# A two-layer decoder kernel: the first layer's expert weights loaded once each, and copied into one working block for every tile of tokens

## What is computed

```python
# E = 8 experts, TOP_K = 2, D = 256, H = 512, x: 2048 tokens of 256
logits = x @ Wg                       # [tokens, 8]
w, pick = softmax over the two largest logits of each token
y = sum over the two picks k:  w[k] * ( (silu(x @ W1[e]) * (x @ W2[e])) @ W3[e] ),  e = pick[k]
out = layernorm(x + y)
```

## Time and profile before

| what | value |
|---|---|
| median of 3 runs | 1277.59 us (1275.09 to 1281.85) |
| the profiled execution, its own time | 1270.34 us |
| its span, first to last instruction | 1268.3 us |
| TensorE busy | 1009.9 us (80%) |
| VectorE, ScalarE, GpSimd busy | 578.7 us, 356.5 us, 228.8 us |
| bytes moved by DMA | 129.22 MB |
| granted TensorE clock, mean | 0.892 of full speed |

### The profile page before, as it was taken

The page is one execution under the profiler, slowest core; times in us unless marked ns, Lnnn a source line. Parts: engine busy times, 40 slices in busy tenths (PEclk is TensorE's granted clock), DMA queues, the critical chain, the costliest instruction groups (busy, mean ns, idle before and its releaser), DMA issues.

```text
span 1268.3 us, 19930 instructions
## 1 busy us (share of the span) xinstructions
PE 1009.9 (80%) x8500; PEld 761.2 (60%) x8500; DVE 578.7 (46%) x1328; ACT 356.5 (28%) x491; POOL 228.8 (18%) x234
## 2 busy tenths in 40 slices
PE   6889689889888888887875797988879797974860
PEld 3656566656657777776874564756556474643540
DVE  3544343545683411111113825565473649445227
ACT  2344324433442121111110153242315322430112
POOL 0310210210302222323221010101010110102642
PEclk9899789988988999999997897999699789966995
DMA  5012912012005778767662000200020010004426
GB/s 168 2 38 97 347 42 67 1 38 67 1 1 215 282 282 303 269 249 258 253 254 83 1 6 2 67 2 5 1 67 2 5 34 1 2 1 128 148 90 198
DMA packets 68216, 129.22 MB, mean 102 GB/s; under 512 B 12752, under 2 KB 57696, under 8 KB 63136
## 3 DMA queue, kind: packets, MB, share of 16 engines
q1 hardware_dynamic: 45984, 97.85, 22.5%
q10 hardware_dynamic: 16480, 14.62, 3.6%
q0 software_dynamic: 5664, 15.47, 3.4%
HBM read 94.50 MB, written 33.42 MB: 101 GB/s over the span
## 4 chain that ended last, share of the span: by engine, by line
PE 52%; DVE 22%; DMA 13%; ACT 6%; POOL 2%; issue 2%; SPq 1%; ACTq 1%; DVEq 0%; POOLq 0%
DMA sb_arena<-in_m_w 11%; PE ps L1627 7%; PE ps L1324 6%; PE ps L1443 6%; DVE sb_arena L793 6%; PE ps L1509 4%; PE ps L1419 4%; ACT sb_arena L587 4%; DVE sb_arena L797 3%; PE ps L1637 3%; DVE ps L816 3%; PE ps L1562 3%; PE ps L1465 2%; PE ps L1701 2%; PE ps L1451 2%
## 5 line engine op out<-in xcount | busy, mean ns | idle before, releaser
L1627 PE MATMUL ps<-sb_arena 128*128 128x128 f32 x1248 | 161.1, 284 | 44.0 <-DMA sb_arena<-in_m_w 43.3
L1627 PEld LDWEIGHTS ps<-sb_arena 128*128 128x128 f32 x1248 | 151.4, 198 | 56.9 <-DMA sb_arena<-in_m_w 55.6
L1214 POOL TENSOR_TENSOR sb_arena<-sb_arena,sb_neghalf 128x2 f32<-128x2 f32 x40 | 30.5, 762 | 602.4 <-DVE sb_arena L759 602.4
L587 ACT ACTIVATE sb_arena<-ps 77x2048 f32<-77x2048 f32 (+1 forms) x64 | 118.4, 1875 | 54.6 <-PE ps L1401 42.0
L1324 PE MATMUL ps<-sb_arena,sb_wreg 128*128 128x256 f32 (+1 forms) x512 | 107.9, 363 | 4.6 <-issue 3.8
L1324 PEld LDWEIGHTS ps<-sb_arena,sb_wreg 128*128 128x128 f32 (+1 forms) x512 | 89.2, 195 | 19.7 <-issue 8.3
L1419 PE MATMUL ps<-sb_arena 32*77 32x256 f32 (+1 forms) x1024 | 92.5, 491 | 7.7 <-ACT sb_arena L587 4.9
L1112 DVE COPY sb_arena<-ps 128x256 f32<-128x256 f32 x39 | 16.6, 424 | 161.2 <-PE ps L1621 161.2
L822 DVE RECIPROCAL sb_arena<-ps 128x32 f32<-128x32 f32 x24 | 8.6, 357 | 147.0 <-PE ps L1451 146.0
L1637 PE MATMUL ps<-sb_arena 128*128 128x256 f32 x312 | 73.9, 380 | 0.6 <-ACT sb_arena L688 0.6
L1273 POOL DMA_INDIRECT outs<-sb_arena,sb_idx x39 | 38.3, 983 | 196.4 <-ACT sb_arena L688 196.4
(11 more groups left out here) (228 smaller groups left out, 1710.1 us busy)
## 6 DMA issues: line engine op xcount, KB each, us to landing
sb_arena<-in_m_w SPq DMA_DIRECT2D x39, 1536.0 KB, 7.1
sent<-sb_xres SPq DMA_DIRECT2D x32, 256.0 KB, 2.9
sb_arena<-outs SPq DMA_DIRECT2D x16, 512.0 KB, 5.8
outs<-sb_zeros ACTq DMA_DIRECT2D x1, 6656.0 KB, 32.7
sent<-sb_zeros ACTq DMA_DIRECT2D x2, 2560.0 KB, 12.7
sb_arena<-in_m_w SPq DMA_DIRECT2D x16, 256.0 KB, 3.7
early<-sb_xres SPq DMA_DIRECT2D x12, 256.0 KB, 2.9
sb_arena<-in_xT SPq DMA_DIRECT2D x8, 256.0 KB, 3.3
```

The lines of the kernel that those rows point to most:

```text
L587: nc.scalar.activation(dst, src, ACT.Exp).then_inc(S(f"h_PT{p}"), 1)
L1627: ins = mm(to[:, m * P:(m + 1) * P], w[:, k, m * P:(m + 1) * P], slots0[j % 2].xT[:, k, :], start=(k == 0), stop=(k == KC - 1))
```

## The change

All eight experts' blocks stay in SBUF. `arena` is cut into blocks of 3072 words: eight of them hold the experts (`BLOCKS`, in the order of first use), one (number 6) is the working block from which PE reads every tile's weights, one (number 1) holds the two sets of `xT`, `sil` and `hT`.

- SyncE issues eight loads in a row, each with a register load of the expert's number from `first_i`; the last four wait also for `h_res1`. The second layer's weights follow in one piece after the first tile's W3.
- The table is now made in two parts: `uses()` in `table_early()` ranks the experts by first use (and then come those without a tile), and `blocks_early()`, a new step of the list behind `index`, makes the table of block numbers, `block_i`.
- For every tile ScalarE copies W1 and W3 and VectorE copies W2 from the expert's block into the working block, 1024 words a row each, with a register load of the block's number ahead of each copy. The copy of W1 for tile j+1 waits until PE has done W1(j), that of W2 until W2(j) is done, that of W3 for tile j until W3(j-1) is done. PE waits for `t_c1`, `t_c2` and `t_c3` in place of the DMA.
- The first copies wait until the last pair's result has been copied away (`store` at 8), as do VectorE's first steps of the mixture.
- Two small constants (`expert_no`, `blocks`) are loaded at the start, on ScalarE's queue.

```diff
-WBUFS = 3
+WORDS = 3072
+BLOCKS = (2, 3, 4, 0, 7, 8, 9, 5)
+EARLY_BLOCKS = 4
+WORK, ROWS = 6, 1
...
-                           "res": [("index",)], "rstd": [("gather",)]} if last else {})
+                           "res": [("index",), ("blocks",)], "rstd": [("gather",)]} if last else {})
...
             sp.wait_ge(S("h_res0"), X0.at(PAIRS))
             sp.wait_ge(S("placed"), 1)
-            for j in range(WBUFS):
-                load_weights(j)
+            sp.wait_ge(S("table"), 1)
+            for k, blk in enumerate(BLOCKS):
+                if k == EARLY_BLOCKS:
+                    sp.wait_ge(S("h_res1"), X0.at(PAIRS))
+                e = sp.value_load(first_i[0:1, k:k + 1], min_val=0, max_val=E - 1)
+                sp.dma_start(arena[:, WORDS * blk:WORDS * (blk + 1)], dram["m0_w"][bass.ds(e, 1), :, :].rearrange("e p a -> (e p) a")
+                             ).then_inc(S(f"landed{k}"), 16)
             for p in range(2):
                 send(p, PAIRS - 1, 0)
-            later = [n for n, _ in attn_items("s1") + attn_items("x1")]
-            for j in range(TILES0 - 2):
-                if j + WBUFS < TILES0:
-                    sp.wait_ge(S("t_y"), j + 1)
-                    load_weights(j + WBUFS)
-                if later:
-                    load_weight(sp, later.pop(0), "c_weights")
+            sp.wait_ge(S("t_y"), 1)
+            for n, _ in attn_items("s1") + attn_items("x1"):
+                load_weight(sp, n, "c_weights")
...
+            def weights0(j, part, used, signal):
+
+                if j < E:
+                    act.wait_ge(S(f"landed{j}"), 16)
+                if j:
+                    act.wait_ge(S(used), j)
+                act.wait_ge(S("table"), 3 if j >= SURE else 2)
+                blk = act.value_load(block_i[0:1, j:j + 1], min_val=0, max_val=max(BLOCKS))
+                nc.scalar.activation(arena[:, WORDS * WORK + 1024 * part:WORDS * WORK + 1024 * (part + 1)],
+                                     arena[:, bass.ds(blk * WORDS + 1024 * part, 1024)], ACT.Copy).then_inc(S(signal), 1)
+
+            act.wait_ge(S("store"), B)
+            weights0(0, 0, "t_u", "t_c1")
+            weights0(0, 2, "t_y", "t_c3")
             for j in range(TILES0):
                 gate0(j)
+                if j + 1 < TILES0:
+                    weights0(j + 1, 0, "t_u", "t_c1")
                 if j:
                     outputs0(j - 1)
+                    weights0(j, 2, "t_y", "t_c3")
...
+            def weights0(j):
+
+                if j < E:
+                    dve.wait_ge(S(f"landed{j}"), 16)
+                if j:
+                    dve.wait_ge(S("t_v"), j)
+                blk = dve.value_load(block_i[0:1, j:j + 1], min_val=0, max_val=max(BLOCKS))
+                v.tensor_copy(arena[:, WORDS * WORK + 1024:WORDS * WORK + 2048], arena[:, bass.ds(blk * WORDS + 1024, 1024)]
+                              ).then_inc(S("t_c2"), 1)
+
+            for p in range(2):
+                dve.wait_ge(S(f"logits{p}"), PAIRS)
+            dve.wait_ge(S("store"), B)
             turned0(0)
+            weights0(0)
             for j in range(TILES0):
                 if j + 1 < TILES0:
                     turned0(j + 1)
                 hidden0(j)
+                if j + 1 < TILES0:
+                    weights0(j + 1)
...
-                pe.wait_ge(S(f"t_w{j % WBUFS}"), 16 * (j // WBUFS + 1))
+                pe.wait_ge(S("t_c1"), j + 1)
                 pe.wait_ge(S("t_xT"), j + 1)
-                hidden0(j, w.w1, bank(p, 1), "t_u")
+                hidden0(j, work["w1"], bank(p, 1), "t_u")
                 if j + 1 < TILES0:
                     turn0(j + 1)
                 if j > 1:
                     pe.wait_ge(S("t_h"), j - 1)
-                hidden0(j, w.w2, bank(p, 2), "t_v")
+                pe.wait_ge(S("t_c2"), j + 1)
+                hidden0(j, work["w2"], bank(p, 2), "t_v")
```

92 lines of the change are left out of this document (62 added, 30 removed).

## The result

| | before | after |
|---|---|---|
| median | 1279.72 us (1275.09 to 1284.14, 4 runs) | **1230.59 us** (1228.51 to 1232.86, 4 runs) |
| ratio | | **0.961** (95%: 0.958 to 0.963) |
| the profiled execution | 1270.34 us, span 1268.3 | 1232.01 us, span 1230.2 |
| bytes moved | 129.22 MB | 80.50 MB |
| VectorE, ScalarE busy | 578.7, 356.5 us | 609.2, 438.4 us |

The forecast was 1226 us, 1216 to 1250. The median is 49 us lower than before; the two profiled executions are only 38 us apart, because the one of before was the lowest of its runs. What follows compares the profiled executions unless a median is named.

The account below looks back on a forecast made before the run. The prediction took weight transfers to bound the first layer's tile stage. 56.2 us saved, less 1.2 for the start, 1.0 for VectorE's routing and 2.3 for ScalarE's router work, gave 51.7 us off: 1226 us, range 1216 to 1250.

Parts of the forecast that it names:

- The pace: First layer's 39 tiles: weight transfers set the pace, 7.05 us a tile against 5.52 us without waits.
- What goes, 56.2 us: First layer's tiles: dropping 31 of 39 weight loads shortens the path from 267.8 to 211.6 us.
- Rival D: In the tiles another transfer, such as gathered rows, sets the pace and nothing is won: 1277 us, chance 0.03.
- ScalarE's share, at most 5.10 us a tile: ScalarE per tile: silu, output copy, two weight copies and two register loads sum to 5.10 us, under 5.52.
- Rivals A and B: ScalarE paces the tiles: A, register load 1.5 us, 1247 us, chance 0.16; B, 2.3 us, 1302 us, chance 0.06.
- VectorE's copy, 1.18 us: Each tile's W2 copy on VectorE, 1024 words from SBUF to SBUF, takes 1.18 us.
- Rival C: VectorE's W2 copies collide with GpSimd and each takes 0.95 us longer: 1232 us, chance 0.08.
- VectorE's routing, 1.0 us: Behind tiles 2, 3 and 5, small routing instructions on VectorE no longer fit: 1 us in all, 0 to 3.
- The start, 1.2 us: Before the first tile, table instructions, register load and first copy add 1.2 us, range 1 to 3.
- The landing of the eight loads at nothing: Early tiles: the eight weight loads land no slower than 5.52 us a tile, so they cost nothing.
- What follows W1(38) stays as it is: Everything after the last tile's W1, second layer included, keeps its time.
- The range: Whole kernel: 1216 to 1250 us, some 0.83; the forecast by itself 1216 to 1236 us, chance 0.67.

Follow-up runs that it names:

- the repeat: The changed kernel run again unaltered, on the chip of three later edited kernels: 1233.83 us, ratio 0.965 to the kernel before.
- the kernel with three loads: The kernel before with 36 of its 39 expert weight loads left out, later tiles reusing the three buffers: 1215.14 us, ratio 0.954.

## Why the prediction was right

Forecast and measurement differ by 5 us (1226 and 1230.59), and the mechanism was the one named. That the number came so close is in part luck: between the two traced executions only 38.1 of the 51.7 us are saved. At the medians it is 49.1, because the kernel before was 9.4 us slower at the median than in its trace and the changed one 1.4 us faster, and no term of the prediction says that the change should save more there. In the repeat, beside executions of the kernel before on the same chip, the medians differ by 45.1 us. By its steps:

- **The pace.** "The stage goes at the pace of the transfers": shown by the kernel with three loads. A tile without a wait was read as 5.52 us, and the changed kernel has 5.52 us in its steady part, at a granted clock of 1.00.
- **What goes, 56.2 us.** From the first W1 to that of tile 38 the kernel before takes 267.84 us and the changed one 619.35 - 399.86 = 219.49: 48.4 us off, where 56.2 less the 1.0 and 2.3 for the routing, 52.9, were predicted. This term failed by 4.5 us. 3.7 of them are the gathered rows of tile 4 and 0.7 those of tile 6, a queue that I had not followed: GpSimd's scatter stands ahead of the next gather, the rows take some 7 us beside the eight loads, and the tiles of 7.05 us had hidden what tiles of 5.52 us do not. The picks cost 2.5 us, where the prediction had read 0.40 us and a wait of 0.64 (1.1 in the kernel with three loads, so 1.4 are the copies beside them); the router's tile cost 1.2 us against 2.3 taken. Rival D, that the gathered rows pace the tiles, was true of these two places alone.
- **ScalarE's share, at most 5.10 us a tile.** Right, with 0.60 + 0.38 + 2 x 1.06 busy (1.05 taken for a copy). The register load, taken at 0.76 to 1.01 us, takes 0.69 to 0.71 with its arithmetic and shows as 0.09 and 0.33 us, because it overlaps the instruction ahead of it. Rivals A and B are out as the pace of the tiles: 0.7 is far from 1.22 and 1.99 us. One load of the 78 did take 1.16 us, at 419.49; 1.00 us shows behind it, and TensorE was waiting for the gathered rows at the time. The Trainium skill, "DMA: Bandwidth & Descriptors", section "Latency and other measured facts", has a floor of about 600 ns under a `tensor_load`; ScalarE's took 277 ns at the median and VectorE's 304, so the measurement decides against it here.
- **VectorE's copy, 1.18 us.** It takes 0.69 us: the rate of 1 ns a word that I had from shorter forms does not hold for it. Nothing followed, since VectorE has room. Rival C is out as a cost: the longest of 39 copies took 696 ns. It was hardly put to the test, though. GpSimd's two instructions of a tile fall between the copies (498.80 and 500.09, with copies at 497.17 and 502.68), and only 2 of the 39 copies meet one at all; in the kernel with VectorE's loads twice one copy began within a scatter's instruction and took 0.69 us, and that instruction 1.30 in place of 0.98. What had made L765 slow before was other work of GpSimd: 16 of its 80 instructions took 673 ns or more, and each of them began within 0.1 us behind the start of a GpSimd instruction on SBUF, as the first of these two did:

```profile
1101.06 1.27 POOL L1226 TENSOR_TENSOR sb_arena<-sb_arena,sb_wreg 128x512 f32<-128x512 f32 x1
1101.13 1.68 DVE L765 TENSOR_SCALAR sb_arena<-sb_arena 128x256 f32<-128x256 f32 x2 [0.27 <-POOL sb_arena L1214]
```

  The Trainium skill, "GPSIMD Engine Reference", section "1. Specifications", names contention of the two engines at SBUF for some VectorE instructions; these 16 agree with it, and the 39 copies say next to nothing about it.
- **VectorE's routing, 1.0 us.** The third, fifth and sixth distance, where it lies, show next to nothing of it (5.52, 5.51, 5.65).
- **The start, 1.2 us.** It was 2.24. The gathers (390.57 against 389.47) and the end of the stores (396.83) came as summed. The step that was off is the one from the stores to the first register load: in ScalarE's order the copy of the last logits stands between them, which by the prediction's own 397.2 ends later than the stores, and which ended at 397.99, 3.1 us later than before where 1.1 + 1.3 were taken; 2.7 of them are the delay of the last normalising by the tables (391.61 against 388.94). Only behind it can ScalarE load its register and copy the first weights:

```profile
397.81 0.18 ACT L608 ACTIVATE sb_logits<-ps 128x16 f32<-128x16 f32 x1 [1.52 <-PE ps L1555]
398.75 2.00 ACT L702 ACTIVATE sb_arena<-sb_arena 128x1024 f32 x2 [0.75 <-issue]
```

- **The landing of the eight loads at nothing.** Right for the weights: no tile waited for one.
- **What follows W1(38) stays as it is.** Wrong twice. The last W3 waits 1.94 us for its copy, 1.4 more than before, since on ScalarE the output copy and the register load stand ahead of it. And the last mixture has 6 us of a stall; that the second layer's stage grows is what the prediction's last sentence had named as a sign of being wrong, without pricing it.
- **The range.** Its inner part, 1216 to 1236, does not follow from the bracket behind it. With the one-time costs, VectorE's and ScalarE's at nothing the sum gives 1277.6 - 56.2 = 1221.4 us, and with all at their upper ends and the landing late 1233.4.

The account in the two profiled executions: 48.4 less 2.2 for the start and 1.4 for the last W3 leaves 44.8 us, and the second layer's first transposes do stand 44.9 us earlier (687.55 and 642.67). Less 6.9 in the last mixture (88.2 and 81.3) gives 38.0, and the spans differ by 38.1 us. Against that the prediction had 51.7. The medians say 49.1; 9.4 us of the difference between 38.1 and 49.1 lie in the executions of the kernel before, whose medians of four runs and more are 1274 to 1280 us where the profiled one had 1270.34, and 1.4 in the changed kernel's. Where in the kernel those 9.4 us arise no trace shows, since the kernel before was traced once; on one chip its executions went from 1262.02 us at a mean granted clock of 0.895 to 1278.27 at 0.880.

## What to carry to other kernels

Where TensorE waits for transfers that bring the same data again, keep them in SBUF and copy; to price it, add up each copying engine's round from its own rows and compare it with the time of a tile without waits, counting a register load only as far as it is longer than the instruction ahead of it. When a stage is made faster, follow every queue that runs one tile ahead, not only the one that waited: the next one late was a gather that stood behind a scatter, and turning the two round was free. Take the time that a transfer needs from rows with the new traffic beside it: this gather took 2.7 us without weight loads and 7.2 with them. Look for the places where the new work has no cover: before the first tile, beside steps that occur once, and after the last.

## What was not expected of the hardware

- A register load on ScalarE or VectorE (277 and 304 ns) with its arithmetic (152 and 190 ns) runs while the engine's earlier instruction computes: 0.09 us show behind a silu of 0.60 us, and four loads in a row begin even ahead of the silu.
- From SBUF to SBUF, 1024 words a row, VectorE copies in 0.69 us and ScalarE in 1.06 us.
- One wait of 1.89 us can cost 3.7 us, as the product behind it takes 3.58 us in place of 1.95, at a granted clock of 0.51; behind a wait of 1.49 us at the same place in another kernel the clock stayed at 1.00.
- A VectorE instruction of 407 ns took up to 1353 ns where it began just behind a GpSimd instruction on SBUF.
- A stall of some 6 us in untouched code, in which TensorE's signals stand up to 3.4 us behind the end of its products; its cause is open, and all five traces that have it lack semaphore events.
